# One matrix engine's small sum moved to GpSimd, with the steps behind it one to three blocks later

## The reference

```python
v = (x - group_mean) / sqrt(group_var + 1e-5)           # 32 groups of 16 channels
h = relu((mean(v) @ fc_w.T - abn_m) * (abn_g / sqrt(abn_v + EPS)) + abn_b)      # 32 hidden values
ch_att, fl_att = sigmoid(h @ ch_w.T + ch_b), sigmoid(h @ fl_w.T + fl_b)          # 512 each
kn_att = softmax(h @ kn_w.T + kn_b)                      # 4 kernels
agg_w = einsum('bk,koc->boc', kn_att, weight)            # a 512x512 matrix of the sample's own
y = einsum('bchw,boc->bohw', v * ch_att, agg_w) * fl_att
out = x + (y - bn_m) * bn_g / sqrt(bn_v + EPS) + bn_b
```

## Time and profile before

| | |
|---|---|
| time, median of 3 runs | 2082.37 us (2082.26 to 2083.61) |
| span of the profiled execution | 2080.4 us |
| TensorE matmul busy, share of the span | 2049.3 us, 99% (10874 instructions) |
| DVE busy | 1879.3 us, 90% |
| ACT busy | 1724.8 us, 83% |
| GpSimd busy | 16.5 us, 1% |
| DMA | 422 MB, 203 GB/s in the mean |
| granted TensorE clock | 1.000 |

### The profile page before, as it was taken

How to read it: one execution, slowest core, us unless ns; L and a number is a source line. 1 busy time by engine, 2 the same in 40 slices (tenths; PEclk the granted TensorE clock), 3 DMA queues, 4 the chain that set the end, 5 groups by cost and what they waited for, 6 DMA issues and landing times.

```text
span 2080.4 us, 33022 instructions
## 1 busy us (share of the span) xinstructions
PE 2049.3 (99%) x10874; PEld 1064.1 (51%) x10874; DVE 1879.3 (90%) x2980; ACT 1724.8 (83%) x2294; POOL 16.5 (1%) x27
## 2 busy tenths in 40 slices
PE   4999999999999999999999999999999999999999
PEld 2555555555555555555555555555555555555554
DVE  8999999999999999999999999999999999999974
ACT  5888888888888888888888888888888888888885
POOL 1100000000000000000000000000000000000000
PEclk9999999999999999999999999999999999999999
DMA  9976665565655656556566555565565655566522
GB/s 370 282 214 204 204 204 202 194 206 202 210 194 194 212 194 212 195 203 202 197 209 203 198 198 205 201 206 200 195 207 198 212 194 198 198 205 210 177 107 106
DMA packets 239646, 422.47 MB, mean 203 GB/s; under 512 B 7553, under 2 KB 237441, under 8 KB 239105
## 3 DMA queue, kind: packets, MB, share of 16 engines
q1 hardware_dynamic: 235920, 415.67, 58.3%
q0 software_dynamic: 3696, 6.42, 1.9%
HBM read 216.55 MB, written 211.94 MB: 206 GB/s over the span
## 4 chain that ended last, share of the span: by engine, by line
PE 98%; DVE 1%; ACT 0%; DMA 0%; issue 0%; SPq 0%; DVEq 0%; ACTq 0%
PE product L920 32%; PE product L921 32%; PE product L919 32%; DVE chunk_stats L487 1%; PE product L948 0%; DMA x_ring<-x 0%; PE small L886 0%; ACT x_norm L365 0%; DVE mixed_weight L673 0%; DVE w_lo L684 0%; ACT w_hi L387 0%; DVE w_lo L738 0%; PE product L941 0%; DVE mean_var L500 0%; SPq L240 0%
## 5 line engine op out<-in xcount | busy, mean ns | idle before, releaser
L919 PE MATMUL product<-x_hi,w_hi 128*128 128x448 f16 x3552 | 1251.9, 352 | 0.0
L920 PE MATMUL product<-x_lo,w_hi 128*128 128x448 f16 x3552 | 1251.9, 352 | 0.0
L921 PE MATMUL product<-x_hi,w_lo 128*128 128x448 f16 x3552 | 1251.9, 352 | 0.0
L329 ACT ACTIVATE y<-product,out_bias,out_scale 128x448 f32<-128x448 f32 x892 | 639.2, 717 | 275.9 <-PE product L921 273.2
L308 ACT ACTIVATE x_norm<-x_ring,norm_bias,norm_scale 128x448 f32<-128x448 f32 x888 | 665.5, 750 | 0.0
L514 DVE TENSOR_TENSOR x_ring<-x_ring,y 128x896 f32<-128x896 f32 x432 | 463.6, 1084 | 96.9 <-ACT y L329 96.0
L919 PEld LDWEIGHTS product<-x_hi,w_hi 128*128 128x128 f16 x3552 | 350.1, 99 | 321.7 <-issue 0.2
L921 PEld LDWEIGHTS product<-x_hi,w_lo 128*128 128x128 f16 x3552 | 347.6, 98 | 324.4
L920 PEld LDWEIGHTS product<-x_lo,w_hi 128*128 128x128 f16 x3552 | 347.6, 98 | 321.5
L479 DVE BATCH_NORM_STATS2 chunk_stats<-x_ring 128x6 f32<-128x448 f32 x868 | 476.7, 612 | 2.5 <-DMA x_ring<-x 0.3
L508 DVE TENSOR_TENSOR x_lo<-x_norm,x_hi 128x1792 f16<-128x1792 f32 x222 | 447.8, 2017 | 21.9 <-ACT x_hi L317 21.9
(11 more groups left out here) (99 smaller groups left out, 330.4 us busy)
## 6 DMA issues: line engine op xcount, KB each, us to landing
x_ring<-x SPq DMA_DIRECT2D x217, 896.0 KB, 4.8
out<-x_ring SPq DMA_DIRECT2D x216, 896.0 KB, 3.8
out<-y SPq DMA_DIRECT2D x7, 896.0 KB, 6.4
out<-x POOLq DMA_DIRECT2D x7, 896.0 KB, 11.4
x_ring<-x SPq DMA_DIRECT2D x12, 448.0 KB, 7.7
weight<-wt SPq DMA_DIRECT2D x4, 1024.0 KB, 16.4
x_ring<-x SPq DMA_DIRECT2D x4, 224.0 KB, 7.2
out<-x_ring SPq DMA_DIRECT2D x4, 224.0 KB, 2.5
```

The source lines that it names most:

```text
L329: nc.scalar.activation(y[:, s % 2, t], acc[k % BANKS][:, 0:COLS], ACT.Identity, bias=obias[:, t:t + 1], scale=oscale[:, u, t:t + 1]).then_ ...
L919: nc.tensor.matmul(bank, whi[:, u, o, t], hi, start=(t == 0), stop=False)
L920: nc.tensor.matmul(bank, whi[:, u, o, t], lo, start=False, stop=False)
L921: ins = nc.tensor.matmul(bank, wlo[:, u, o, t], hi, start=False, stop=(t == CT - 1))
```

## The change

From the third sample on, `hidden` on TensorE goes. GpSimd instead waits for `fc_sums` and does a `partition_all_reduce` of it into a new SBUF tile `hidden_sum`: a sum over the 128 partitions, left on all of them. DVE's `logits` waits for that and reads it in place of the PSUM tile. The first two samples keep the matmul. In both tables of places, the steps behind it come later:

| step | engine | before | after |
|---|---|---|---|
| `logits` | DVE | (3,3) | (4,0) |
| `exponentials` | ACT | (4,0) | (4,1) |
| `attentions` | DVE | (4,1) | (4,2) |
| `first_mix` | ACT | (4,1) | (4,2) |
| `mix_kernel` | DVE | (4,2), (5,0), (5,1) | (5,0), (5,1), (5,2) |
| `split_weight`, `w_hi` | ACT | (5,2) | (5,3) |
| `split_weight`, `w_lo` | DVE | (5,3), (6,0) | (6,0), (6,1) |

```diff
+ReduceOp = bass.bass_isa.ReduceOp
...
+        hid_sum = sb("hidden_sum", [P, HIDDEN])
...
+        hid_summed = sem("hid_summed")
...
@@ act
-                usual = {"guess": (3, 0), "exp": (4, 0), "mix": (4, 1), "split": (5, 2)}
+                usual = {"guess": (3, 0), "exp": (4, 1), "mix": (4, 2), "split": (5, 3)}
...
@@ dve
-            def logits(turn, b):
-
-                dve.wait_ge(hid_done, turn.at(2, b + 1))
-                step(nc.vector.tensor_tensor(hid[:, 0:HIDDEN], hid_p, hbias[:, :], ALU.add))
+            def logits(turn, b, summed_by_pool=False):
+
+                if summed_by_pool:
+                    dve.wait_ge(hid_summed, turn.at(2, b - 1))
+                else:
+                    dve.wait_ge(hid_done, b + 1)
+                step(nc.vector.tensor_tensor(hid[:, 0:HIDDEN], hid_sum[:, :] if summed_by_pool else hid_p,
+                                             hbias[:, :], ALU.add))
...
-                usual = {"means": (2, 0), "mean": (2, 1), "var": (3, 0), "norms": (3, 1), "logits": (3, 3),
-                         "att": (4, 1), "mix": [(4, 2), (5, 0), (5, 1)], "split": {(5, 3): (0, 1), (6, 0): (2, 3)}}
+                usual = {"means": (2, 0), "mean": (2, 1), "var": (3, 0), "norms": (3, 1), "logits": (4, 0),
+                         "att": (4, 2), "mix": [(5, 0), (5, 1), (5, 2)], "split": {(6, 0): (0, 1), (6, 1): (2, 3)}}
...
-                                logits(turn, b)
+                                logits(turn, b, not (first and b == 1))
...
@@ pool, behind the residual DMAs of the first sample
+            for b in range(2, B):
+                pool.wait_ge(pooled_ready, b + 1)
+                nc.gpsimd.partition_all_reduce(hid_sum[:, :], fcs[:, :], P, ReduceOp.add).then_inc(hid_summed, 1)
...
@@ pe
-                        if prepare and (n, o) == ((4, 1) if first and b == 1 else (3, 2)):
+                        if first and b == 1 and (n, o) == (4, 1):
                             hidden(turn, b)
```

## The result

| | before | after |
|---|---|---|
| time, median | 2082.92 us | 2185.53 us (2184.23 to 2185.79, 5 runs) |
| ratio | 1 | 1.0492, 95% interval 1.0481 to 1.0503 |
| span of the profiled execution | 2080.4 us | 2184.0 us |
| mean granted TensorE clock | 1.000 | 0.984 |

The account below looks back on a forecast made before the run. TensorE was taken as the bound (98% of the span). A new stall of 2.4 us less 0.14 saved, 2.27 us over 30 samples, gave 68 us more: 2150.5 us, range 2090 to 2230.

Parts of the forecast that it names:

- Bound and gain: TensorE is 98% of the span; removing 30 matmul sums saves 0.14 us a sample, 4.2 us in all.
- The all-reduce: On GpSimd, 0.25 to 8.0 us long, taken as hidden before VectorE's logits, 6.5 us after `fc_sums`; cost zero.
- Steps 1 to 6: Moved steps laid out on VectorE and ScalarE, ending in a TensorE stall of 2.4 us at a sample's start.
- steps 5 and 6: `x_hi` of chunk 7 behind `w_hi`: VectorE waits 2.0 us; last two `w_lo` behind `x_lo`: TensorE stalls 2.4 us.
- step 1: Second add of chunk 3 on VectorE, now ahead of the logits, waits 0.5 us for the evacuation of (3,3).
- Steps 2 to 4: Later attentions and first mix step; VectorE waits 1.6 us at chunk 4's second add; `w_hi` starts 3.1 us later.
- The check by waits: VectorE gets 4.1 us of new waits for 0.9 old, ending 3.1 to 3.2 us later against 0.78 us cover.
- Does the lag carry over: Whether one sample's delay grows into the next; claimed no, each sample pays once.
- Shut out: Rival: the all-reduce on GpSimd holds VectorE up for its whole length, 4 us: 2255 us; chance 0.12.
- Long: Rival: an all-reduce of 8.0 us makes VectorE wait 1.6 us at the logits: 2198 us; chance 0.08.
- Half of it: Rival: only the 1.6 us wait at chunk 4's second add is absent, stall 0.8 us: 2102 us; chance 0.10.
- no stall: Rival: TensorE's gap at a sample's start stays shut, so only the gain remains: 2078 us; chance 0.08.

Follow-up runs that it names:

- e2: Kernel before with the sum on GpSimd from the third sample on, all steps left at the old places: 2078.97 us.
- e4: Changed kernel with all four `w_lo` at (6,0), ahead of `x_lo` of the next sample's first chunk: 2109.63 us.
- e5: Changed kernel with the four `w_hi` on ScalarE moved from (5,3) to (6,0), behind `x_hi` of the next sample's first chunk: 2109.54 us.
- e8: Changed kernel with three `w_lo` at (6,0) ahead of `x_lo` and one behind it at (6,1): 2131.72 us.
- e7: Kernel before with the sum on GpSimd and only the logits one block later, at (4,0): 2086.79 us.
- e3: Changed kernel with 16 unread fp16 matmuls on TensorE at the start of each sample but the first, ahead of its waits: 2153.43 us.
- e6: Changed kernel with the all-reduce done twice, the first into a spare tile nobody reads: 2183.67 us.
- e9: Old places with the sum on GpSimd, plus three more all-reduces ahead of the one that is read: 2105.82 us.
- e10: Changed kernel with GpSimd holding the all-reduce until both adds of chunk 3 are done, so it runs beside VectorE's statistics: 2183.58 us.
- e1: Kernel before with only the new places of the steps; the sum stays the fp32 matmul on TensorE: 2194.25 us.

## Why the prediction was right, and where its sum fell short

- **Bound and gain.** Right. e2 gives 3.7 us for 30 sums where 4.2 were summed; a sample takes 63.56 us there against 63.70.
- **The all-reduce.** Hidden, as taken. It is out at 1080.90, 4.1 us before VectorE reads it at 1085.04; 2.31 us lies between the bounds of 0.25 and 8.0, and its own 0.53 us near the lower one. The estimate of 3.9 us that the prediction set beside them was too high.
- **Steps 1 to 6.** Right to some 0.1 us. Laid out plus 50.40 against measured: second add of chunk 3 1081.9 (1081.91); logits 1085.0 (1085.04); second add of chunk 4 1092.05 (1092.03), waits 1.6 (1.49); third mix step to 1102.9 (1102.85); `x_lo` 1107.1 (1107.06), wait 2.0 (1.89); last `w_lo` 1110.46 (1110.41); TensorE starts 1110.6 (1110.63). e4, e5 and e8 confirm steps 5 and 6 one by one, and e7 shows the wait of step 1 (0.40 us) by itself. Steps 2 to 4 were seen in the trace and not tried alone. Two side figures were off by little. The 0.15 us for release and weight load, which no row of before showed, are 1110.63 - 1110.41 = 0.22 us here. The check by waits gave 3.1 to 3.2 us; its own waits came out at 0.40 + 1.49 + 1.89 = 3.8 us for 0.9 of old, so 2.9, and the steps, which give 3.0, are the better of the two.
- **Does the lag carry over.** Right: 28 pauses are 2.42 to 2.45 us, the last two 2.28 and 2.12; none grows.
- **The term that was missing.** The forecast's 68 us are measured as 30 x 2.30 = 69. What failed is the last sentence of the prediction, the lower clock behind a pause "priced at nothing": it costs 20 x 1.69 = 34 us, and 69 + 34 = 103 is the difference of the medians (102.6). e3 takes out the clock and nothing else and gives 32 of the 34 back. The error was to forecast a new pause on TensorE thirty times over and not to give it the price of what may follow it; nothing in the trace of before showed either, as it has no pause of that size at full stream. It should have stood among the bounds: half clock doubles the 0.19 us of a matmul for as long as it lasts.
- **Luck.** For its own chain the prediction gave 2135 to 2160 us, and 2185.5 is outside that. It is inside 2090 to 2230 only because the upper end made room for a long all-reduce or one that shuts VectorE out, and neither is what happened.
- **Rivals.** *Shut out* falls (e6: adds and `x_lo` unchanged); the 0.3 us of loss where two instructions meet, read from L684, doesn't show with an all-reduce either. *Long* falls by length, though e9 shows that its mechanism is real. *Half of it* and *no stall* fall; e2 shows that no stall is what the old places give.
- **The rule of the Trainium skill** ("SBUF — State Buffer", Who interferes with whom), which I had as a rival with a chance of 0.12: e10 agrees with one side of it. The all-reduce takes 0.53 us beside statistics with one SBUF input and 2.31 beside `x_lo` with two, so GpSimd's read waits for VectorE. The other side, VectorE waiting for GpSimd, doesn't show with the all-reduce: the instruction with two inputs had always started first. But the rows of before that the prediction held against the rule show it, read one by one:

```profile
36.69 1.24 POOL L867 TENSOR_SCALAR x_norm<-x_ring,norm_scale,norm_bias 128x448 f32<-128x448 f32 x1
37.43 0.64 DVE L684 SCALAR_TENSOR_TENSOR w_lo<-mixed_weight,channel_att_scaled,w_hi 128x128 f16<-128x128 f32 x1
...
37.92 0.84 POOL L867 TENSOR_SCALAR x_norm<-x_ring,norm_scale,norm_bias 128x448 f32<-128x448 f32 x1
...
38.26 0.64 DVE L684 SCALAR_TENSOR_TENSOR w_lo<-mixed_weight,channel_att_scaled,w_hi 128x128 f16<-128x128 f32 x1
...
38.75 1.30 POOL L867 TENSOR_SCALAR x_norm<-x_ring,norm_scale,norm_bias 128x448 f32<-128x448 f32 x1
...
39.55 0.64 DVE L684 SCALAR_TENSOR_TENSOR w_lo<-mixed_weight,channel_att_scaled,w_hi 128x128 f16<-128x128 f32 x1
```

Each of the three `w_lo` steps of 0.64 us starts while a TENSOR_SCALAR is under way and ends 0.14 us after it (38.07 against 37.93, 38.90 against 38.76, 40.19 against 40.05). So they waited for its end, as far as the rough spans of GpSimd can show it, and lost 0.3 us each; no run was made to try it. The prediction looked for the loss of a whole TENSOR_SCALAR, but only its rest can be lost by a step that comes late to it. So *shut out* fell because the all-reduce came second and is short, and not because GpSimd can't hold VectorE up.

## What to carry to other kernels

Where one engine is at 99% and two others at 83% and 90%, what counts of a moved step is the order in the queues: list what now stands behind what, and lay it out with the old start-to-start spacings. Here that gave each of seven times to 0.1 us. Before steps are moved to make room for a slower operation, measure the operation where it stands: this one fitted with 0.5 us to spare. And once a pause on TensorE is forecast, price the clock behind it as well; a few matmuls in the pause are a quick way to see its share.

## What the runs showed of the hardware

- TensorE's clock, from 2.4 to 1.2 GHz: with a pause of 2.43 us (between stretches of 63 to 65 us without any) it fell behind 20 pauses of 30, and behind 22 of 30 in e1, for some 3.4 us, at a price of 1.69 us. In the kernel after, the fall came 0.6 us behind a pause, then 1.2 us behind the next, then not at all, and so on in turn; in e1 0.2, 0.6, 1.0 us and not at all. With pauses of 1.01, 1.03 and 1.78 us it never fell in 30 each, nor with a pause of 0.53 us behind 1.9 us of filler. What makes one of three equal pauses harmless stays open.
- A `partition_all_reduce` of 128x32 fp32 takes 0.53 us beside one-input instructions of VectorE, 1.11 beside an add of 128x896 and 2.31 beside the `x_lo` subtraction of 2.02 us. The prediction had taken 0.25 to 8.0.
- With the all-reduce, GpSimd waiting for VectorE is all the contention there was: VectorE's adds and `x_lo` kept their lengths within 3 ns in the mean. With GpSimd's TENSOR_SCALARs of the first sample, VectorE waits too, 0.3 us a `w_lo` step (L684).
